# A language model's attention and routing stage: softmax sums inverted by ScalarE and GpSimd, routing quarters at other slots, last tail interleaved

## What is computed

```
# attention, x is the layer-normalised hidden state; 16 heads of 32
S = K Q^T * SCALE, -inf above the diagonal, minus the distance i - j
C = softmax(S)                    # exp(S - row maximum) / sum of its row
hidden += (C V) @ o_w.T + o_b
# experts: E = 32, the K = 6 best, at most CAP = 192 rows to an expert
h = layernorm(hidden)
scores = sqrt(softplus(h @ gate_w.T));  idx = top_k(scores + bias, 6)
w = 1.5 * scores[idx] / sum(scores[idx])
pos = number of earlier rows that chose the same expert (cumulative count)
routed = sum over the six of w * expert(h)                # rows with pos < CAP
shared = clip(silu(h @ sg.T) * (h @ su.T), -10, 10) @ sd.T
out = hidden + routed + shared
```

## Time and profile before

| | us |
|---|---|
| median of 3 runs | 3865.16 |
| lowest and highest | 3862.11, 3866.61 |
| the profiled execution | 3872.97 |
| its span | 3871.2 |
| PE busy in it | 3245.3 (84%) |
| DVE, POOL, ACT busy | 2419.5 (63%), 1671.2 (43%), 1112.7 (29%) |
| one period of the loop over batches | 382.3 (1145.7 to 1528.0) |
| PE busy in that period | 339.27 |
| tail after the last batch | 3325.55 to 3520.07 |

### The profile page before, as it was taken

One profiled execution on the slowest core, in us unless ns is written; L12 is line 12 of the kernel. 1 busy time (PEld: TensorE's weight loads), 2 busy tenths in 40 slices (PEclk: granted clock), 3 DMA queues, 4 the chain that ended last, 5 costly groups with the idle time before them and its releaser, 6 DMA issues. The chain is left out here.

```text
span 3871.2 us, 62509 instructions
## 1 busy us (share of the span) xinstructions
PE 3245.3 (84%) x20296; PEld 1670.1 (43%) x20296; DVE 2419.5 (63%) x6622; ACT 1112.7 (29%) x2553; POOL 1671.2 (43%) x924
## 2 busy tenths in 40 slices
PE   4647999888888888888888888889888977655998
PEld 2324444444444444444444444444444433334776
DVE  6733565567667665766576657665776577553554
ACT  3751333233223322332233223322332233101111
POOL 5630354445435443544454445444444446322332
PEclk8878999999999999999999999999999988867999
DMA  5664000021111011101010101010101000104996
GB/s 199 244 271 136 1 28 20 28 77 50 68 51 46 14 34 34 34 12 39 29 34 12 40 28 34 12 40 28 34 12 39 28 12 12 55 25 133 259 259 154
DMA packets 123205, 257.87 MB, mean 67 GB/s; under 512 B 38988, under 2 KB 39628, under 8 KB 120192
## 3 DMA queue, kind: packets, MB, share of 16 engines
q1 hardware_dynamic: 78400, 201.42, 15.8%
q0 software_dynamic: 44048, 49.26, 5.0%
q10 hardware_dynamic: 432, 3.15, 0.2%
HBM read 146.71 MB, written 204.26 MB: 91 GB/s over the span
## 5 line engine op out<-in xcount | busy, mean ns | idle before, releaser
L806 POOL TENSOR_TENSOR a_first_probs<-a_first_probs,a_probs 128x2048 f32<-128x2048 f32 (+3 forms) x320 | 1033.5, 3230 | 1594.1 <-ACT a_probs L872 1375.0
L994 DVE CUSTOM_DVE_ANT_0 a_unused<-a_ps_ring,a_decay 128x512 bf16<-128x512 f32 (+3 forms) x1536 | 773.4, 554 | 515.8 <-PE a_ps_ring L1285 510.2
L872 ACT ACTIVATE a_probs<-a_ps_ring 128x512 f32<-128x512 f32 (+3 forms) x1280 | 505.5, 473 | 794.8 <-PE a_ps_ring L1319 600.1
L810 POOL DMA_INDIRECT d_slots<-a_rows,a_place_i x397 | 395.6, 997 | 226.3 <-DVE a_place_i L1147 141.7
L1309 PE MATMUL a_ps_ring<-a_k_t,a_q_t 32*128 32x512 f32 (+3 forms) x3072 | 412.6, 539 | 72.4 <-DVE a_row_max L994 44.0
L1285 PE MATMUL a_ps_ring<-a_q_t,a_k_t 32*128 32x512 f32 (+3 forms) x3072 | 391.3, 542 | 17.5 <-DVE a_row_max L994 12.6
L1383 PE MATMUL a_ps_dense<-a_sd,a_inner_t 128*128 128x512 f32 x256 | 184.5, 860 | 191.3 <-DVE a_gate_up L1127 188.0
L1273 PE MATMUL a_ps_dense<-a_normed_t,a_q_w 128*128 128x512 f32 x512 | 246.0, 625 | 35.1 <-DVE a_max_cols L980 32.5
L872 ACT ACTIVATE a_first_probs<-a_ps_ring 128x512 f32<-128x512 f32 x256 | 135.6, 605 | 475.8 <-PE a_ps_ring L1319 450.9
L1332 PE MATMUL a_ps_heads<-a_probs,a_values 128*32 128x512 f32 (+3 forms) x2560 | 269.9, 495 | 0.0
L1309 PEld LDWEIGHTS a_ps_ring<-a_k_t,a_q_t 32*128 32x128 f32 x3072 | 146.0, 186 | 274.9 <-issue 147.0
(11 more groups left out here) (177 smaller groups left out, 4402.2 us busy)
## 6 DMA issues: line engine op xcount, KB each, us to landing
d_hidden<-e_hidden SPq DMA_DIRECT2D x8, 2048.0 KB, 7.9
d_normed_t<-e_normed_t SPq DMA_DIRECT2D x8, 2048.0 KB, 11.6
a_normed_t<-d_normed_t SPq DMA_DIRECT2D x8, 2048.0 KB
a_residual<-d_hidden SPq DMA_DIRECT2D x64, 256.0 KB
d_hidden<-a_residual SPq DMA_DIRECT2D x64, 256.0 KB
a_hidden<-d_hidden SPq DMA_DIRECT2D x64, 256.0 KB
out<-a_hidden SPq DMA_DIRECT2D x64, 256.0 KB
x_w_gate<-w_gate SPq DMA_DIRECT2D x32, 512.0 KB, 6.3
```

The costliest lines, as they stand in the source:

```text
L806: nc.gpsimd.tensor_tensor(total_of, total_of, probs_of(m)[:, :, 0:width], ALU.add).then_inc(added, 1)
L810: nc.gpsimd.indirect_dma_start(slot_rows, bass.IndirectOffsetOnAxis(ap=place_i[p][:, j, choice:choice + 1], axis=0), rows[p][:, j, :], Non ...
L872: nc.scalar.activation(probs_of(m)[:, h, 0:width], score_bank(m, h)[:, 0:width], ACT.Exp).then_inc(exp_done, 1)
L994: nc.vector.tensor_tensor_reduce(unused[:, h, 0:width], row_bank(k, h)[:, 0:width], decay[:, at:at + width], 1.0, NEG, ALU.add, ALU.max, r ...
```

## The change

- *Sums.* The ones by which PE sums are minus ones, so the sums come negated. ACT takes the logarithm (Ln of minus the input) into `sum_inv` and a plain copy into `inner_t`, which is free there and is used under the name `minus_sum`; later in the same slot the exponential of minus the logarithm, a guess of the inverse (`take_sums`, `guess_inverse`). DVE makes one Newton step of it, x(2 - sx), as two operations of 128x512 (`invert_sums`) in slot 2 or 6, and POOL multiplies the heads (`multiply_heads`), one operation of 128x512 in slot 3 or 7 ahead of that slot's addition.
- *Evictions.* `take_values` and `take_maxima` are on ACT. So is the gate's addition of 1 (Identity with a bias).
- *Small ones.* Counts are kept in bf16 and added inside `find_places`; `place` is four small matmuls in place of two. A few pairs of DVE operations are fused.
- *Quarters.* For g = 1 to 3 the quarter's uses stand at other slots; g = 0 keeps them. PROJECT_AT changes with them. For g > 0 slot 6 has no use of the bank, gap (7, C) has two (`up` 1, then a projection), and so has (10, C) for g = 2 and 3 (`down` 1, then a projection). Statistics, normalising, softplus, root, choice, count and gates move one slot ahead for g > 0.
- *Prologue.* The first batch's tokens are loaded in two halves, and PE starts with the first. The biases come on ACT's queue. PE doesn't wait for the other constants until it turns the first maxima. SP starts the transfers that fill the experts' slots only behind PE's prologue.
- *Last tail.* The uses go round four banks (those of the ring of scores), each with semaphores of its own, in an order written out in `late_uses`. The residual is loaded into eight tiles during the last step and stays there. Rows have four buffers.

The tables and the new functions:

```diff
-              1: ((0, C), (1, C), (2, C), (3, C), (7, C), (9, C)),
-              2: ((1, C), (2, C), (3, C), (4, C), (7, C), (9, C)),
-              3: ((0, C), (1, C), (2, C), (3, C), (7, C), (9, C))}
+              1: ((0, C), (1, C), (2, C), (5, C), (7, C), (8, C)),
+              2: ((1, C), (2, C), (5, C), (7, C), (10, C), (11, C)),
+              3: ((0, C), (1, C), (2, C), (5, C), (7, C), (10, C))}
...
-QUARTER_AT = ((("turn", 0), 4, A), (("turn", 1), 4, B), (("route", 0), 5, C), (("up", 0), 6, C), (("up", 1), 8, C),
-              (("place", 0), 10, C), (("down", 0), 11, A), (("down", 1), 11, C))
+QUARTER = (("turn", 0), ("turn", 1), ("route", 0), ("up", 0), ("up", 1), ("place", 0), ("down", 0), ("down", 1))
+QUARTER_AT = {True: ((4, A), (4, B), (5, C), (6, C), (8, C), (10, C), (11, A), (11, C)),
+              False: ((3, A), (3, B), (3, C), (4, C), (7, C), (9, C), (10, A), (10, C))}
...
-LATE_DIVIDE, EARLY_DIVIDE = (1, 2, 3, 4), (6, 8, 9, 10)
+LATE_INVERT, EARLY_INVERT = 2, 6
...
+    uses = out(0, 0) + out(0, 1) + [("sums", 1, None)] + turn(0, 0) + turn(0, 1)
+    for q in range(QUARTERS):
+        uses += [("route", 0, q), ("up", 0, q)] + out(q + 1, 0) + [("up", 1, q)] + out(q + 1, 1) + [("place", 0, q)]
+        uses += turn(q + 1, 0) + turn(q + 1, 1) + [("down", 0, q), ("down", 1, q)]
...
-            sp.dma_start(normed_t[:], dram["normed_t"][0]).then_inc(normed_in, 16)
+            sp.dma_start(normed_t[:, :, 0:HALF], dram["normed_t"][0, :, :, 0:HALF]).then_inc(normed_half_in, 16)
+            sp.dma_start(normed_t[:, :, HALF:T], dram["normed_t"][0, :, :, HALF:T]).then_inc(normed_in, 16)
...
+            sp.wait_ge(dense_full, N_PROLOGUE)
...
+            def multiply_heads(s, g, half):
+
+                heads = attn_t[:, g, half_cols(half)]
+                pool.wait_ge(heads_taken, 2 * s + half + 1)
+                pool.wait_ge(sums_inverted, 2 * s + half + 1)
+                nc.gpsimd.tensor_tensor(heads, heads, sum_inv[half][:], ALU.mult).then_inc(heads_done, 1)
...
-                nc.scalar.activation(sum_inv[half][:], ps_dense[:], ACT.Identity).then_inc(dense_free, 1)
+                nc.scalar.activation(sum_inv[half][:], use.bank[:], ACT.Ln, scale=-1.0).then_inc(sums_log, 1)
+                nc.scalar.activation(minus_sum, use.bank[:], ACT.Identity).then_inc(use.free, 1)
+
+            def guess_inverse(s, half):
+
+                act.wait_ge(sums_log, 2 * s + half + 1)
+                nc.scalar.activation(sum_inv[half][:], sum_inv[half][:], ACT.Exp, scale=-1.0).then_inc(sums_guessed, 1)
+
+            def take_maxima(p, half, use):
+
+                act.wait_ge(use.full, use.n + 1)
+                nc.scalar.activation(row_shift[p][:, half_cols(half)], use.bank[:], ACT.Identity).then_inc(use.free, 1)
...
+            def soften_gate(x, m, use):
                 if m > 0:
                     act.wait_ge(inner_done, MC * x + m)
...
+            def invert_sums(s, half, use):
+
+                dve.wait_ge(sums_guessed, 2 * s + half + 1)
+                dve.wait_ge(use.free, use.n + 1)
+                nc.vector.tensor_tensor(minus_sum, minus_sum, sum_inv[half][:], ALU.mult).then_inc(newton, 1)
+                dve.wait_ge(newton, 2 * s + half + 1)
+                nc.vector.scalar_tensor_tensor(sum_inv[half][:], minus_sum, 2.0, sum_inv[half][:],
+                                               ALU.add, ALU.mult).then_inc(sums_inverted, 1)
...
-                chain.done(nc.vector.tensor_scalar(gate_e[:], gate_e[:], 1.0, None, ALU.add))
-                chain.wait()
                 chain.done(nc.vector.reciprocal(gate_e[:], gate_e[:]))
```

More of the change, by code:

```diff
@@ L491, in plan @@
     if tail:
-        for use, slot, gap in QUARTER_AT:
-            put((slot, gap), use)
+        for use, at in zip(QUARTER, QUARTER_AT[g == 0]):
+            put(at, use)
     if projects:
@@ L651, in attend, with late, dense @@
         N_CONSTS = len(consts) + 3
-        N_MADE = 3
+        N_MADE = 2
         FREE = 16
         SCATTERS = 16 * 2 * TOPK
-        TAIL_STEPS = 49
+        NORM_STEPS, TAIL_STEPS = 8, 35
+        @dataclass
+        class Use:
+            bank: object
+            full: object
+            free: object
+            n: object
+        def late(kind, arg, q=None):
+            n = next(n for n, (k, a, u) in enumerate(LATE) if (k, a) == (kind, arg) and (q is None or u == q))
+            k = n % LATE_BANKS
+            return Use(ps_ring[k], late_full[k], late_free[k], n // LATE_BANKS)
+        def dense(n):
+            return Use(ps_dense, dense_full, dense_free, n)
         def shape(m):
@@ L872, in soften, with take_values @@
                 nc.scalar.activation(probs_of(m)[:, h, 0:width], score_bank(m, h)[:, 0:width], ACT.Exp).then_inc(exp_done, 1)
+            def take_values(g, half, use):
+                act.wait_ge(use.full, use.n + 1)
+                nc.scalar.activation(values[g][:, half_tiles(half), :], use.bank[:].rearrange("p (t m) -> p t m", m=P),
+                                     ACT.Identity).then_inc(use.free, 1)
             def take_heads(s, g, half, outs_through=None):
@@ L1028, in take_stats, with take_late_stats @@
+            def take_late_stats(q, norm):
+                for j in range(2):
+                    use = late("out", 2 * q + j)
+                    dve.wait_ge(use.free, use.n + 1)
+                take_stats(late_hidden[2 * q:2 * q + 2], norm)
+            def take_stats(tiles, chain):
                 dve.wait_ge(tail_consts_in, 16 * len(tail_consts))
                 for j in range(2):
-                    dve.wait_ge(hidden_in[j], 16 * (x + 1))
-                    chain.done(nc.vector.bn_stats(stats[:, j, :], hidden[j][:]))
+                    chain.done(nc.vector.bn_stats(stats[:, j, :], tiles[j]))
@@ L1076, in soft_sum @@
                 chain.wait()
[L1077 to L1079 removed]
+                nc.vector.scalar_tensor_tensor(soft[:], soft[:], SOFT_LEAST, plus[:], ALU.max, ALU.add).then_inc(soft_done, 1)
             def choose(x, chain):
@@ L1162, in gate, with add_shared @@
                 nc.vector.tensor_scalar(inner_t[:, m, :], gate_e[:], LIMIT, -LIMIT, ALU.min, ALU.max).then_inc(inner_done, 1)
-            def add_shared(j, n):
-                dve.wait_ge(dense_full, n + 1)
-                nc.vector.tensor_tensor(hidden[j][:], ps_dense[:], hidden[j][:], ALU.add).then_inc(dense_free, 1)
-            def take_dense(st, slot, gap, chains):
+            def add_shared(tile, use):
+                dve.wait_ge(use.full, use.n + 1)
+                nc.vector.tensor_tensor(tile, use.bank[:], tile, ALU.add).then_inc(use.free, 1)
@@ new lines, in tail_events @@
+            def tail_events(st, m, norm, chain):
+                x, first = QUARTERS * st.t + st.g, st.g == 0
+                if m == STATS_AT[first]:
+                    for j in range(2):
+                        dve.wait_ge(hidden_in[j], 16 * (x + 1))
+                    take_stats([tile[:] for tile in hidden], norm)
+                if m == NORMALISE_AT[first]:
+                    dve.wait_ge(rows_free, x + 1)
+                    normalise(x, rows[st.g % 2], [tile[:] for tile in hidden], norm)
+                if m == SOFT_SUM_AT[first]:
@@ L1233, in quarter @@
                 count_chosen(chain)
-                gate(x, 1, epilogue_use(q, "up", 1), chain)
-                find_places(q % 2, epilogue_use(q, "place", 0), chain)
+                if more:
+                    normalise_late(q + 1, norm)
+                gate(x, 1, late("up", 1, q), chain)
+                find_places(q, late("place", 0, q), chain)
                 for j in range(2):
-                    add_shared(j, epilogue_use(q, "down", j))
-            for n, (kind, half) in enumerate(PROJECTIONS * 2):
-                if kind == "v":
-                    take_values(n // N_PROJ, half, n)
-                if n >= N_PROJ:
-                    for k in range(2):
-                        row_maxima(0, 2 * (n - N_PROJ) + k)
+                    add_shared(late_hidden[2 * q + j], late("down", j, q))
@@ L1252, in _ @@
+            norm = norm_chain(0)
+            take_late_stats(0, norm)
+            invert_sums(FINAL - 1, 1, late("sums", 1))
+            normalise_late(0, norm)
             for q in range(QUARTERS):
@@ L1392, in count_earlier @@
                                  start=True, stop=False)
-                nc.tensor.matmul(ps_dense[:, 0:2 * E], ones_b[:], counts_b[:].rearrange("p j e -> p (j e)"),
-                                 start=False, stop=True).then_inc(dense_full, 1)
-            def of_quarter(x, p, kind, arg, n):
+                for j in range(2):
+                    nc.tensor.matmul(use.bank[:, j * E:(j + 1) * E], ones_b[:], counts_b[:], start=False, stop=False)
+                nc.tensor.matmul(use.bank[:, E:2 * E], ones_b[:], chosen_b[:, 0, :], start=False, stop=True).then_inc(use.full, 1)
```

521 lines of the change are left out of this document (275 added, 246 removed).

## The result

The changed kernel takes 4118.16 us (median of 4 runs, 4117.82 to 4118.34), the kernel before 3865.89; the ratio is 1.0648, with a 95% interval of 1.0631 to 1.0665. The forecast was 3841, faster. The profiled execution has a span of 4116.5 us.

What follows compares the result with a forecast made beforehand. PE, busy 84%, was taken as the bound. From 3872.97 us: +5.9 per batch times 7 = +41, first batch +9, tail -63, prologue -11 give 3849, minus 7.8 = 3841; range 3715 (0.08 below) to 3960 (0.10 above).

Steps and rivals of the forecast that it cites:

- The ends: Before and after the loop: earlier first projection, -11 us (0 to -20); overlapped quarters after the last batch, 131 for 194.5, -63.
- full collision: Upper end of each new wait: DVE's products held by POOL's additions, from old rows laid end to end in new order.
- first rival: Collisions slip past: lighter DVE reaches its products before POOL's additions; 3646 us, or 3728 with maxima as laid; chance 0.15.
- (e): Slot 7's bank used twice, projection waiting for ACT behind gate 0: 0.96 to 3.1 us, middle 2.0, three times, +6.1 per batch.
- (f): Place waits for the count's products behind additions of groups 8 and 9: none or 3.20 in two quarters, middle +3.2 per batch.
- (a): Division leaves DVE, so PE's wait at "down" shrinks from 25.8 us to four times 3.2: -13.0 per batch.
- (b): Values evicted by ACT, which waits for PE there, so waits of 4.6 + 1.6 us vanish: -6.2 per batch.
- (c): Maxima's eviction on ACT queues behind logarithm, copy, exponentials and guess, delaying PE's projections: +10.5 us per batch, lower end 0.
- (d): Turn a slot earlier in three quarters: normalising can be stopped by POOL; nothing to 6.7 us, middle +3.4 per batch.
- (g): A projection right behind "down 1" in two quarters, a plain double use of the bank, 0.96 us each: +1.9 per batch.
- slower rival: Additions hold gate 0 in slot 7; 3960 us with all collisions full, 4009 with lower clock, +7 each; chance 0.34.
- the second: The slower case: turn, slot 7 and place all collide with POOL's additions, +22.9 us per batch, 3960 or 4009; chance 0.34.

Runs made afterwards that it cites:

- e6: The changed kernel with the quarters' old slots, and division, maxima and values' evictions on DVE as before; 3753 us, ratio 0.9701 against the kernel before.

## Why the prediction was wrong

- *The ends* were right. Prologue -11, measured -12; tail -63, measured -63 (131 us, a quarter 31). e6 shows them alone, with a loop that also gained.
- *The step that failed* is the rule "Of each new wait I take the middle between its uncovered minimum and the full collision that I get by laying the rows of before end to end in the new order; no row decides between them". Rows did decide: POOL's addition comes at a fixed place of a slot, as the prediction says itself against its first rival, so each collision happens in every batch or in none. The collisions of (e) and (f) all happened, 19 waits behind up 1 (5.4 to 5.6 us) and 13 at place (6.4 to 6.5) in the whole run. Second, the full collision as laid out was too small, since each was laid alone: nothing held the inversion (2.63 for 0.7), and nothing delayed POOL's product and the addition behind it until the reciprocal was nearly over. Only two-operand work was let stand still; the count's conversions and the gate's limit (and its addition, before), of one operand, stood still as well.
- *(a) Down*: forecast 12.8 us a period, measured 18.7, of which 13.7 are there with short additions.
- *(b) Values*: gone, as forecast. But with the values on DVE, in e6, all but 1.0 us of the wait is gone too, so the stated reason isn't what was needed.
- *(c) Maxima*: forecast +10.5, measured 4.1 + 3.0 and some 1 elsewhere, about +8. The first batch, +9 by the same argument, lost nothing.
- *(d) Turn*: forecast +3.4, measured 4.2 - 1.1 = +3.1.
- *(e) Slot 7*: forecast 2.0 each and 3.1 in full, measured 5.57. The largest miss of a wait, +10.6 a period.
- *(f) Place*: forecast 1.6 each, 3.2 in full, measured 6.4: another +9.6. Here two collisions follow each other, at the count's first conversion and at its last.
- *(g)*: +1.8, forecast +1.9.
- *The clock* had no term in the sum, and only +7 in the slower rival. PE's busy time measured +21.0 us a period and 132 over the seven batches, two fifths of what these lost. That alone would have turned the sign of the forecast: 3841 + 132 = 3973.
- *Seven times*: the sum takes seven periods of the loop. There are six, at +50 each in place of +5.9, and the last batch, at +22.
- *The rival that came true* is the second, by its mechanism (ACT held by gate 0, held by the addition), at +50 us a period where it had +22.9, or +29.9 with the clock. Its dearest case, 4009, is still 109 us short, and 111 us of the slots' cost are there without long additions and aren't explained in full.

## What to carry to other kernels

When the same instruction of two engines meets at a fixed place of a loop, a collision isn't a matter of chance: lay the two queues out side by side with their durations and take what comes, and lay them out together, since one delay opens the next. Put POOL's long additions where DVE has row maxima or reciprocals to do, and mind what releases POOL: an operation that DVE signals early lets POOL in on the rest of DVE's block (129 us here for one swap). A count of engine time taken off DVE (181 us here) says nothing while the work that is left stands at worse places.

## What was unexpected of the hardware

Small operations were stopped for as long as large ones, and operations of one operand as well: a conversion of 16 columns took 3.92 us beside an addition of 4.52, one of 64 columns 3.53 beside one of 3.45, a limit L1244 up to 2.9. Row maxima and reciprocals kept 0.69 and 1.75 us beside such additions. Nearly all of the period's 82 us at half clock (of 433) begin in or right behind waits of 2.8 to 6.4 us, in stretches of 6.8 to 17.1 us, the longest behind place's waits. Short additions brought the 82 back to 38 with no other change on PE; down's four waits, 3.4 to 3.6 us each there, are still followed by 6.8 us at half clock each.
